# Late low-rank terms, an early copy of down's adapter sums, spread loads, and weight splits inside the quantiser

## The reference

```python
# layer 0: a quantised weight with a low-rank term
delta = lora_B @ lora_A * (32 / 64)                  # 1024 x 1024, rank 64
normalized = (weight + delta) / scale                # scale by group of 128
w = quantise(normalized) * scale                     # 8 levels of a codebook
x = x + x @ (w + delta).T
# layer 1: gated MLP with one adapter out of 16 for each sequence, rank 16
gate = x @ W_gate.T + 0.5 * (x @ A_gate[i].T) @ B_gate[i].T     # 2752 columns
up   = x @ W_up.T   + 0.5 * (x @ A_up[i].T)   @ B_up[i].T
act  = silu(gate) * up
x = x + act @ W_down.T + 0.5 * (act @ A_down[i].T) @ B_down[i].T
```

## Time and profile before

| | |
|---|---|
| median of three runs | 1713.2 us |
| the profiled execution: its time, its span | 1714.91 us, 1713.3 us |
| TensorE busy | 1625.6 us (95%) |
| VectorE busy | 1283.8 us (75%) |
| ScalarE, GpSimd busy | 555.2 us (32%), 520.6 us (30%) |
| mean granted clock of TensorE | 0.978 |
| HBM traffic over the span | 152 GB/s |

### The profile page before, as it was taken

The page is one execution under the profiler, slowest core; times in us unless marked ns, Lnnn a source line. Parts: engine busy times, 40 slices in busy tenths (PEclk is TensorE's granted clock), DMA queues, the critical chain, the costliest instruction groups (busy, mean ns, idle before and its releaser), DMA issues.

```text
span 1713.3 us, 21654 instructions
## 1 busy us (share of the span) xinstructions
PE 1625.6 (95%) x7200; PEld 1327.9 (78%) x7200; DVE 1283.8 (75%) x1744; ACT 555.2 (32%) x983; POOL 520.6 (30%) x399
## 2 busy tenths in 40 slices
PE   6989996999999999996899999999999899999999
PEld 5868884788888888764688888888767688888887
DVE  6789957788888899987888898977665665674342
ACT  5511124233333333342233333333331333233231
POOL 4230011255554555631345555633310000000000
PEclk9999998999999999997999999999999999999999
DMA  7673273266667777682477777644279776465453
GB/s 214 152 133 98 84 198 85 64 155 165 159 168 166 174 187 178 167 254 78 113 162 177 186 178 184 164 111 104 78 195 237 161 191 170 130 192 189 145 179 103
DMA packets 382829, 266.79 MB, mean 156 GB/s; under 512 B 228608, under 2 KB 303360, under 8 KB 382592
## 3 DMA queue, kind: packets, MB, share of 16 engines
q1 hardware_dynamic: 301696, 234.29, 52.6%
q10 hardware_dynamic: 78944, 25.32, 6.3%
q0 software_dynamic: 2080, 5.80, 1.8%
HBM read 169.41 MB, written 90.14 MB: 152 GB/s over the span
## 4 chain that ended last, share of the span: by engine, by line
PE 79%; DVE 13%; DMA 3%; ACTq 2%; issue 2%; SPq 1%; ACT 1%; DVEq 0%
PE bank L1599 20%; PE bankA L1599 14%; PE bankC L1599 13%; PE bank L1830 8%; PE bankA L1830 5%; PE bankC L1830 5%; PE bankT L1830 3%; DVE qsum L1397 2%; ACTq L964 2%; DMA xs<-XR_d 2%; PE bankT L1734 1%; PE bankT L1645 1%; PE bankT L1646 1%; PE bankC L1612 1%; DVE xl L1165 1%
## 5 line engine op out<-in xcount | busy, mean ns | idle before, releaser
L908 ACT CAST rh<-wt 128x512 fp32r<-128x512 f32 (+1 forms) x308 | 187.9, 611 | 512.9 <-PE bankA L1612 124.4
L1156 DVE TENSOR_TENSOR rl<-wt,rh 128x512 fp32r<-128x512 f32 (+1 forms) x308 | 275.8, 901 | 9.5 <-ACT rh L908 9.5
L1296 DVE TENSOR_TENSOR ll<-ll,lh 128x512 fp32r<-128x512 f32 (+1 forms) x154 | 105.7, 689 | 170.7 <-ACT lh L976 170.1
L1599 PE MATMUL bank<-xh,rh 128*128 128x512 f32 (+1 forms) x528 | 207.3, 393 | 0.0
L1599 PE MATMUL bank<-xl,rh 128*128 128x512 f32 (+1 forms) x528 | 207.2, 393 | 0.0
L1599 PE MATMUL bank<-xh,rl 128*128 128x512 f32 (+1 forms) x528 | 207.0, 392 | 0.0
L976 ACT CAST lh<-ll 128x512 fp32r<-128x512 f32 (+1 forms) x154 | 95.0, 621 | 306.7 <-DMA ll<-LT_d 209.6
L775 POOL TENSOR_TENSOR wt<-wt 128x512 f32<-128x512 f32 (+1 forms) x44 | 56.6, 1287 | 318.8 <-DVE wt L1150 318.8
L1599 PE MATMUL bankC<-xh,rh 128*128 128x512 f32 (+1 forms) x352 | 138.0, 392 | 0.0
L1599 PE MATMUL bankC<-xl,rh 128*128 128x512 f32 (+1 forms) x352 | 137.9, 392 | 0.0
L1599 PE MATMUL bankC<-xh,rl 128*128 128x512 f32 (+1 forms) x352 | 137.8, 392 | 0.0
(11 more groups left out here) (204 smaller groups left out, 3709.9 us busy)
## 6 DMA issues: line engine op xcount, KB each, us to landing
ll<-LT_d SPq DMA_DIRECT2D x140, 256.0 KB, 2.9
wn<-in_L_cond_W_gate_dram SPq DMA_DIRECT2D x80, 256.0 KB, 5.3
wn<-in_L_cond_W_up_dram SPq DMA_DIRECT2D x80, 256.0 KB, 5.1
RT_d<-dt SPq DMA_DIRECT2D x70, 256.0 KB, 3.1
ql<-RT_d SPq DMA_DIRECT2D x70, 256.0 KB, 3.6
LT_d<-ev ACTq DMA_DIRECT2D x60, 256.0 KB, 2.5
dn<-in_L_cond_W_down_dram SPq DMA_DIRECT2D x86, 128.0 KB, 3.8
LT_d<-s2a SPq DMA_DIRECT2D x40, 256.0 KB, 4.1
```

Of the source, the lines that this page charges most:

```text
L908: nc.scalar.copy(rh[:, v % RING, 0:KH * rows], wsrc(RSRC[p], rows)).then_inc(s_hi, 1)
L1156: dv.tensor_tensor(rl[:, v % RING, 0:KH * rows], wsrc(RSRC[p], rows), rh[:, v % RING, 0:KH * rows].bitcast(f32), ALU.subtract).then_inc(s_ ...
L1296: dv.tensor_tensor(ll[0:rows, n % NL, :], ll[0:rows, n % NL, :].bitcast(f32), lh[0:rows, n % NL, :].bitcast(f32), ALU.subtract).then_inc(s ...
L1599: last = te.matmul(OUT[p][0:rows, :], a[:, u % RING, cols], b[:, OPND[p], k, :], start=first and k == ks[0] and n == 0, stop=k == KH - 1 a ...
```

## The change

- The low-rank matmuls of each half's first matrix move: products 2 and 5 get theirs after product 5, products 4 and 6 after product 1 of the next matrix. They count on a semaphore of their own, `s_sl`. `T(h, 1)` moves from ahead of product 4 to ahead of product 6 and into `bank1`. On VectorE `make_ts(h, 0)` moves from p = 2 to p = 3 and `make_ts(h, 1)` to the end of p = 6, and the evictions move behind the terms (function `take`). `x_hi` and `x_lo` of the second half come one product later. `silu` of the half's first tile comes later, and `store_bs` of its second tile too.
- `take_td` takes all four blocks out of `bankT` in four instructions, and `make_td` does the rest after it, both where the first half's sums are made (mm = 23) and in down; step 11 waits for `take_td` alone. The last four `td` come one step later. The four `bd` loads are issued at steps 9, 12, 15 and 18, `td2` at 19 and `bdn` at 24 (before: 9, 13 and 22).
- In layer 0 `w_lo` and `adapters_lo` of block o stand inside `quantise(o + 1)`, after its sixth instruction, and `lb_lo` near its end (for block 2 inside `quantise(1)`). `lora_delta(o + 2)` goes ahead of `w_groups(o + 1)`, `lb_group(o + 2)` ahead of `main(o, 0)`; for block 2 both stand between the matmuls of chunks 0 and 1. Its load is issued after the sixth load of x.

```diff
+        def bankB(o):
+            return bankY[1] if o == 2 else bankL
...
+                    if g == 0 and it % NJ == 1:
+                        sp.wait_ge(s_sl, 4 * (it // NJ + 1))
...
                 for n in range(2, 2 * NC):
                     load_nat(n)
-                sp.wait_ge(s_trL, 2)
-                load_lb(2)
+                    if n == 5:
+                        sp.wait_ge(s_trL, 2)
+                        load_lb(2)
...
-                        for i in range(4):
-                            sp.dma_start(bd[i * CR:(i + 1) * CR, :, :].bitcast(f32),
...
+                    if n in (9, 12, 15, 18):
+                        i = n // 3 - 3
+                        sp.dma_start(bd[i * CR:(i + 1) * CR, :, :].bitcast(f32),
...
                     if n == 13:
                         store_td(1)
+                    if n == 19:
                         sp.wait_ge(s_tdst, 16 * NC)
...
+                    if it % NJ == 0:
+                        if (m, p) == (0, 6):
+                            silu(it, 0)
+                        if (m, p) == (1, 2):
+                            silu(it, 1)
+                            silu(it, 2)
...
+                def take_td(h):
...
+                    for t in range(2):
+                        dv.tensor_copy(td_s[rows[2 * t], :], bankT[rows[2 * t + 1], :]).then_inc(s_mk, 1)
+                    for t in range(2):
+                        mine = rows[2 * t]
+                        dve.wait_ge(s_mk, base + t + 1)
+                        dv.tensor_tensor(td_s[mine, :], bankT[mine, :], td_s[mine, :], ALU.add).then_inc(s_mk, 1)
...
                     chain(at_step(2))
+                    mid()
...
+                    late()
                     n = QS - 6
...
+                def mid_of(o):
+                    w_lo(o - 1)
+                    if o == 1:
+                        lb_lo(2)
+                    else:
+                        adapters_lo(o - 2)
...
+                    if mm in (0, NM // 2) and p == 3:
+                        make_ts(mm // (NM // 2), 0)
...
+                        if mm in (0, NM // 2):
+                            if p == 5:
+                                take(mm, 2)
+                                take(mm, 3)
+                            if p == 6:
+                                make_ts(mm // (NM // 2), 1)
+                        elif p in (2, 3, 4, 6):
+                            if mm in (1, NM // 2 + 1) and p == 2:
+                                take(mm - 1, 4)
+                                take(mm - 1, 6)
+                            take(mm, p)
...
-                    if special and p == 4:
+                    if special and p == 6:
                         T(h, 1)
                     pe.wait_ge(s_lo, u + 1)
                     if special:
                         pe.wait_ge(s_xlo, 2 * (7 * h + p + 1))
+                        if p == 5:
+                            pe.wait_ge(s_tc, 8 * h + 2)
+                    if mm in (1, NM // 2 + 1) and p == 0:
+                        pe.wait_ge(s_tc, 8 * h + 6)
...
+                    product(u, special or p in (0, 1, 3))
+                    if special:
+                        if p == 5:
+                            lora(u - 3, s_sl)
+                            lora(u, s_sl)
+                    elif p in (2, 4, 5, 6):
+                        lora(u, s_pd)
+                    if mm in (1, NM // 2 + 1) and p == 1:
+                        lora(u - 4, s_sl)
+                        lora(u - 2, s_sl)
```

More of the change, by code:

```diff
@@ L1036, in _ @@
                         nat_lo(XFIRST + KD * c + k, NX)
+                        if c == 0 and k == 2:
+                            lb_hi(2)
                     out_x1(c)
-                lb_hi(2)
                 w_hi(1)
@@ L1237, in make_ts @@
                     ins.then_inc(s_ts, 1)
-                def make_td(h, t):
-                    base = MK * (2 * h + t)
+                def take_td(h):
+                    base = 2 * MK * h
+                    rows = [slice(i * CR, (i + 1) * CR) for i in range(4)]
                     dve.wait_ge(s_tdm, 4 * NJ * (h + 1))
@@ L1351, in _, with quantise @@
                 settle(dv.reciprocal(rscale[:, :, :].rearrange("p o g -> p (o g)"), scale[:, :, :].rearrange("p o g -> p (o g)")))
-                def quantise(o):
+                def quantise(o, mid, late):
                     base = QS * o
@@ L1575, in _ @@
                         r_lo(r_ // 2 + 1, k_)
-                    if n in (7, 8):
-                        make_td(1, n - 7)
+                    if n == 8:
+                        take_td(1)
+                    if n in (9, 10):
+                        make_td(1, n - 9)
                     if r > 0 and k in (0, 2, 4, 6):
@@ L1590, in _, with product @@
                 OPND = (R11, T2, R21, T3, T1, T4, R22)
-                def product(u, ks, first, signal):
+                def product(u, signal):
                     mm, p, it, m = split(u)
                     rows = rows_of(it % NJ)
-                    last = None
-                    for k in ks:
+                    for k in range(KH):
                         cols = slice(k * rows, (k + 1) * rows)
@@ L1599, in product @@
                             last = te.matmul(OUT[p][0:rows, :], a[:, u % RING, cols], b[:, OPND[p], k, :],
-                                             start=first and k == ks[0] and n == 0,
+                                             start=k == 0 and n == 0,
                                              stop=k == KH - 1 and n == 2 and p in (0, 1, 3))
@@ L1612, in lora @@
                     te.matmul(OUT[p][0:rows, :], bs[:, m, t, half * rows:(half + 1) * rows], ts[:, t, m, :],
-                              start=False, stop=True).then_inc(s_pd, 1)
+                              start=False, stop=True).then_inc(signal, 1)
                 def T(h, t):
@@ L1753, in _ @@
                 for o in range(KD - 1):
+                    if 0 < o < KD - 2:
+                        lb_group(o + 2)
                     main(TURN[o, 0])
```

181 lines of the change are left out of this document (90 added, 91 removed).

## The result

| | before | after |
|---|---|---|
| median of 4 runs each, in one series | 1712.8 us (1711.1 to 1714.7) | 1700.3 us (1699.4 to 1701.2) |
| span of the profiled execution | 1713.3 us | 1698.4 us |
| TensorE busy | 1625.6 us | 1624.2 us |
| TensorE idle (span less busy) | 87.7 us | 74.2 us |

The ratio is 0.993, with a 95% interval of 0.991 to 0.994. The change makes the kernel faster by 12.5 us (15 in the profiled executions), where 33 were forecast; 1700.3 lies above the range (1667 to 1697 at its widest). At 0.7% it is small, but clear of the spread of the runs.

What follows compares the result with a forecast made beforehand. It took TensorE, busy 95% of the span, as the bound, with only idle time and slow stretches to win. Terms 12.4 + 14 + 8 - 1 = 33.4 us off 1714.9 gave 1681.5, as median 1680 us; range 1667 to 1697.

Steps and rivals of the forecast that it cites:

- The bound and the first half: TensorE bounds the kernel; at the first half's start waits go and the next matrix's first product comes 12.4 us nearer.
- The second half: At the second half's start `make_ts` starts earlier and TensorE gains 14 us, bounds 8 and 20.
- the wait for `ad`: At the second half's second matrix TensorE waits for VectorE's `ad` 8 us instead of 6.3.
- VectorE is the bound at both starts: Rival at both halves' starts: TensorE gives gains back at following gates, half of 26.4 us goes, 1693 us; chance 0.15.
- Layer 0: Layer 0 starts block 1 11 us late, regains 8.5 and 2, and ends with a loss of 1; bounds -6 and +5.
- The 8.5 and 2 to be regained: In layer 0, 8.5 us from the wait at 97.28 and its slow matmuls, 2 from later blocks' `quantise` waits.
- Down: In down the wait of 4.07 us at `bankT` goes with its slow matmuls; 8 us booked, bounds 3 and 15.7.
- what is late next is the residual: In down ScalarE's issuing of residual loads holds up the operand casts behind them, stopping TensorE again for 4 us.
- down loses nothing: Rival in down: the deferred loads take both waits away, 1673 us; chance 0.10.
- The slower rival: Rival in down: deferred `bd` and `td2` loads delay eight residuals by 7.33 us each, 59 us, 1739 us; chance 0.04.

Runs made afterwards that it cites:

- xback: The changed kernel with `x_hi` and `x_lo` of the second half one product earlier, as before the change: 1699.1 us, ratio 0.993.
- lb3: The changed kernel with the load of block 3's low-rank factor issued ahead of the stores of chunks 0 and 1: 1694.3 us, ratio 0.990.
- wlo: The changed kernel with `w_lo(0)` ahead of `quantise(1)` as before, and `lb_lo(2)` near the end of `quantise(1)`: 1689.9 us, ratio 0.987.
- oldrespre: The kernel before the change, only with the residual copied into its arrangement during gate and up, ahead of down: 1704.8 us, ratio 0.996.
- gpres: The changed kernel with GpSimd instead of ScalarE issuing the residual's loads, the same eight DMAs a tile: 1702.2 us, ratio 0.993.
- bdold: The changed kernel with the four `bd` loads together at step 9 and `td2` at 13, as before: 1697.2 us, ratio 0.991.
- bdlate: The changed kernel with `bd` loads at steps 21, 23, 25, 27, `td2` at 22 and the scaling of `bd` at 30: 1697.0 us, ratio 0.990.

## Why the prediction was wrong, step by step

**The bound and the first half: right.** No wait is left inside products 3 and 5. The stop ahead of product 5 is 4.8 us (3.6 forecast), `ts` is ready at 297.4, just as product 5 ends, a stop of 1.7 follows for the last operand, which VectorE ends at 299.80 (second row; the third names no releaser), and the next matrix's first product is 12.0 us nearer (12.4 forecast). The walk of both engines with measured durations gave the number; that it came within 0.4 is partly luck, since this stage took 30.3 us, not 31.9, in seven of the other kernels that left it alone.

```profile
292.37 0.77 PE L1653 MATMUL bankC<-xh,rh 128*128 128x512 f32 x1 [4.80 <-DVE tx L1278]
...
297.44 2.36 DVE L1185 TENSOR_TENSOR xl<-xr,xh 128x1024 fp32r<-128x1024 f32 x2
...
299.91 0.61 PE L1682 MATMUL bank<-xh,at 128*128 128x512 f32 x1 [1.70 <-issue]
```

**The second half: wrong by 6.** The failed step is "`x_lo` comes one product later, so VectorE, which at 771.15 was splitting operand 5, can start `make_ts` there". The splits moved by one product, and `make_ts` moved by one product too, so operand 4 now stands where operand 5 had stood, a lo part and a transpose follow it, and `make_ts` starts no earlier. On the same scale (the copy of mm = 22 came at 762.78 and now at 755.90, 6.9 earlier) 771.15 is 764.3 after; it started at 770.39, 6.1 later than that. It took 8.7 us, not 7.9. The distance from the half's first product to the next matrix's fell by 8.5 where 16 was forecast; of the wait for `ad` after it the forecast was right (7.6 for 8). xback shows that this order isn't the cause by itself: with operand 5 split first the stretch is as long. What is left is the one that I gave as the rival "VectorE is the bound at both starts" and held at 0.15; it fits the second start only. There VectorE is busy 94% of 85 us, and its timeline shows no idle time from 744 to 790 us; in the first start it still stood 3.6 us ahead of the split at 277.64. Part of that busy time is stretching beside GpSimd: the instructions at 754.41, 764.38 and 771.84 and a lo part of 1.78 us (0.68 elsewhere) took some 6.5 us more than their like with GpSimd idle, an estimate from these rows. No run took GpSimd's work away, so how much of the stop of 10 is its share stays open.

**Layer 0: wrong by 5.6, a loss of 6.6 where the bound was 6.** (The terms add up to a loss of 0.5, which was booked as 1.) The first part is mis-sized: `w_lo(0)` was booked at 7.2 and cost 9.3 at the first chunk. The load of the factor was placed rightly behind chunk 1's store, "with everything 8 later and 3 to land", but it was 10.3 later and took 7.4 to land, and the clock fell behind the stop. So block 1 started 18.7 late and not 11. The 8.5 and 2 to be regained were 8.8 and 3.3. lb3 and wlo show both costs singly.

**Down: wrong by 6.3, below its bound of 3.** There is no wait at `bankT`, as forecast, though 3.0 of its 4.1 us go by the residual's repair alone (oldrespre). The failed step is "what is late next is the residual ... I let it be stopped again for 4". It was stopped four times, 12.0 us. I saw the engines at 0.93 and put the delay down to ScalarE's chain of issues, and I took the worth of a deferred megabyte from the mean rate of 221 GB/s. Neither holds: the stops stay at 12.0 us when GpSimd issues (gpres), where `bd` stands changes 3 us (bdold, bdlate), and the eight DMAs in 128-byte pieces cost 14.3 us in the old down (473.3 less 459.0) and 18.8 in the new one, so they swallow 4.5 of the 6.2 us that its changes are worth. The rival "down loses nothing" needed another change. The slower rival (7.33 us at each of eight residuals) decided from 4.2 us a load; measured were 12.0 us over eight, 1.5 each.

The three misses have one sign. Each time I priced the resource behind the wait (VectorE, the DMA that brings the factor, the DMA engines in down) by what it did in the old order, and not by how full it would be in the new one.

## What to carry to other kernels

When two pieces of work on the bound engine are both moved by one step, write down what stands at each place afterwards; a start read from the old trace belongs to the instruction that was there. Before a removed wait is booked as a gain, look at how full the next resource is: here VectorE was busy 0.94 of the stretch and the DMA engines 0.91 from 1250 to 1300 us, and the wait moved on. A slow load is read first by its packets (bytes over count), and only then by who issues it and when.

## What the runs showed of the hardware

- Pieces of 128 bytes take twice the DMA engines' time per byte of rows of 2 KB: 35.1% for 5.16 MB against 19.0% for 5.59 MB in the same 100 us.
- Issuing takes the issuing engine's time, and not the same each time: eight issues on ScalarE took 3.8 and 4.0 us from 1280.18 on and 12.0 at 1289.11. The DMA share doesn't tell them apart, it was 1.1 to 1.2 in all three.
- VectorE instructions are stretched while GpSimd runs: the two TENSOR_SCALAR of `tx` took 2.72 us beside GpSimd's 771.83 to 774.4, and 0.61 at 793.95, with GpSimd idle (first row); before, the four CAST of `ts` took 3.66 us beside its 777.33 to 780.2 and 1.71 at 799.53:

```profile
793.95 0.61 DVE L1281 TENSOR_SCALAR tx<-tx,half_of 64x256 f32<-64x256 f32 x2
...
777.22 3.66 DVE L1231 CAST ts<-tx 32x512 fp32r<-32x512 f32 x4
...
799.53 1.71 DVE L1231 CAST ts<-tx 32x512 fp32r<-32x512 f32 x4
```

- A wait of 5.7 us ahead of `main(0)` cost TensorE 9.3 us at the end of its first chunk, since the matmuls behind it ran near the 1.2 GHz level at first: from 49 to 55 us the granted clock was 0.56 with 27 matmuls made, before it was 1.00 with 43.
